# Tanh-GELU feed-forward stage on Trainium2: cube computed on POOL, curve opened on DVE, excess as half less its clip

## The reference, cut to what matters

```
def _qdot(x, w, out_dtype=BF16):
    return jnp.dot(x.astype(E4M3), w.astype(E4M3), preferred_element_type=out_dtype)
ff_gate = _qdot(x, w_gating[0])        # 256 -> 1024
gate_value = jax.nn.gelu(ff_gate)      # tanh form
ff1 = _qdot(x, w_gating[1])            # 256 -> 1024
activations = gate_value * ff1
outputs = _qdot(activations, w_linear) # 1024 -> 256
```

## Time and profile before

| | us |
|---|---|
| median of three runs | 2270.92 |
| lowest and highest | 2260.33, 2270.98 |
| profiled execution | 2276.07 |
| its span | 2274.3 |

### The profile page before, as it was taken

One profiled execution on the slowest core, in us unless ns is written; L12 is line 12 of the kernel. 1 busy time (PEld: TensorE's weight loads), 2 busy tenths in 40 slices (PEclk: granted clock), 3 DMA queues, 4 the chain that ended last, 5 costly groups with the idle time before them and its releaser, 6 DMA issues. The chain is left out here.

```text
span 2274.3 us, 41972 instructions
## 1 busy us (share of the span) xinstructions
PE 1944.8 (86%) x11782; PEld 1303.9 (57%) x11798; DVE 1366.0 (60%) x3452; ACT 1075.4 (47%) x2800; POOL 717.9 (32%) x691
## 2 busy tenths in 40 slices
PE   7999999998998997776899999979856788988665
PEld 4666666665565665544566666635533457777432
DVE  6555665565775354343533344469879547777687
ACT  5544545553333221111344444357778437666576
POOL 3233333230000023343255556523100016666410
PEclk9999999999999888768999999989978889989887
DMA  9960000000000001142477777500010111111100
GB/s 311 288 188 0 0 0 0 0 1 0 0 0 1 1 27 47 44 161 74 117 167 165 168 175 133 124 1 2 1 58 1 62 36 33 29 35 34 31 17 21
DMA packets 145576, 145.10 MB, mean 64 GB/s; under 512 B 49377, under 2 KB 133569, under 8 KB 145345
## 3 DMA queue, kind: packets, MB, share of 16 engines
q1 hardware_dynamic: 122432, 113.81, 17.4%
q0 software_dynamic: 23040, 30.01, 7.7%
HBM read 137.12 MB, written 66.44 MB: 90 GB/s over the span
## 5 line engine op out<-in xcount | busy, mean ns | idle before, releaser
L1684 POOL DMA_INDIRECT expert_sums<-moe_rows_in,moe_to x128 | 198.0, 1547 | 155.7 <-DMA expert_sums<-moe_rows_in,moe_to 100.1
L1757 PE MATMUL moe_gate<-moe_places,moe_xt 128*128 x512 | 176.3, 467 | 2.3 <-issue 1.9
L1947 DVE COPY moe_ht_e<-moe_turned 128x256 f32<-128x256 f32 x128 | 54.4, 425 | 203.2 <-PE moe_turned L1765 192.5
L619 ACT ACTIVATE ga_prob<-ga_score,ga_neg_max 128x128 f32<-128x128 f32 x256 | 99.6, 390 | 145.9 <-DVE ga_neg_max L493 145.9
L3010 POOL TENSOR_TENSOR wa_low<-wa_low,wa_top 128x512 f32<-128x512 f32 x128 | 133.2, 1041 | 97.3 <-DVE wa_top L3214 96.0
L240 POOL TENSOR_TENSOR ga_q_inv<-ga_q_sum,half 128x4 f32<-128x4 f32 x64 | 64.5, 1008 | 304.2 <-DVE ga_q_sum L476 304.2
L2037 POOL TENSOR_TENSOR ln_rstd<-ln_var,half 128x4 f32<-128x4 f32 (+1 forms) x16 | 21.9, 1370 | 367.5 <-DVE ln_var L2033 367.4
L1151 POOL DMA_INDIRECT slot_x<-early x96 | 94.0, 979 | 137.5 <-DVE early L1144 109.5
L3211 DVE SCALAR_TENSOR_TENSOR wa_low<-wa_score,early 128x512 f32<-128x512 f32 x128 | 87.8, 686 | 60.7 <-PE wa_score L3050 58.1
L375 PE MATMUL ga_summed<-ga_wo,ga_out_t 128*128 128x256 f32 x512 | 122.5, 383 | 0.7 <-ACT ga_out_t L627 0.7
L375 PEld LDWEIGHTS ga_summed<-ga_wo,ga_out_t 128*128 128x128 f32 x512 | 98.1, 192 | 40.6 <-issue 29.2
(11 more groups left out here) (480 smaller groups left out, 4967.8 us busy)
## 6 DMA issues: line engine op xcount, KB each, us to landing
moe_places<-in_L_ffn_packed SPq DMA_DIRECT2D x128, 608.0 KB
slot_x<-zeros SPq DMA_DIRECT2D x24, 1076.0 KB, 15.7
moe_rows_in<-slot_x SPq DMA_DIRECT2D x128, 134.5 KB
wa_v<-v_ctx SPq DMA_DIRECT2D x16, 180.0 KB, 3.0
early<-in_L_xattn_Wq SPq DMA_DIRECT2D x5, 512.0 KB, 7.9
x<-in_x SPq DMA_DIRECT2D x4, 512.0 KB, 9.1
ga_wo<-in_L_xattn_Wo SPq DMA_DIRECT2D x1, 2048.0 KB, 14.1
expert_sums<-zeros SPq DMA_DIRECT2D x2, 1024.0 KB, 8.1
```

What stands on the lines that cost most here:

```text
L619: last = act.activation(prob[:, n % 2, part], score[:, n % 2, part], ACT.Exp, bias=neg_max[:, n % 2, h:h + 1], accum_out=total[:, n % 2, h ...
L1684: pool.indirect_dma_start(out=mem.sums[j % SUMS], out_offset=bass.IndirectOffsetOnAxis(ap=to[:, j:j + 1], axis=0), in_=y[:, j, :], in_offs ...
L1757: last = pe.matmul(both[j % 2][:, 0:2 * FE], xt[:, j % 2, c, :], packed[:, place, c * 2 * FE:(c + 1) * 2 * FE].rearrange("p a n -> p (a n) ...
```

## The change

Three edits, all inside `gelu_ffn`, with the same values computed:

1. The cube is no longer made on DVE but on POOL, by sixteen `tensor_tensor` instructions queued ahead of `norm_next.root`. Each waits for `square` of its step, for `part` of two steps before (which reads the buffer that the cube overwrites), and for `gate` of four steps before. DVE's `part` waits for the new semaphore `cubed`, and so does ACT's square of two steps later.
2. `more` is no longer made on ACT but on DVE, by a `tensor_scalar` with two operations, right before `gate`. ACT's tanh now waits for the `more` of two steps before.
3. The excess is now half less its clip: `within` = min(max(half, -120), 120) in one `tensor_scalar` with two operations, and `over` = half - within as a `tensor_tensor`.

```diff
-        curve = signal("curve", 4)
+        curve, cubed = signal("curve", 3), signal("cubed")
...
             @block.gpsimd
             def _(pool):
+                def cubes(n):
+                    pool.wait_ge(squared.sem, squared.at(n))
+                    if n >= 2:
+                        pool.wait_ge(curve.sem, curve.at(n - 2))
+                    if n >= DEEP:
+                        pool.wait_ge(made.sem, made.at(n - DEEP))
+                    pool.tensor_tensor(cube[:, n % 2, :, :], square[:, n % 2, :, :], g[:, n % DEEP, :, :], ALU.mult).then_inc(cubed.sem, 1)
+
+                for n in range(N):
+                    cubes(n)
                 norm_next.root(pool, 0, 0, B - GROUP)
...
                     if n >= 2:
-                        act.wait_ge(curve.sem, curve.at(n - 2))
+                        act.wait_ge(cubed.sem, cubed.at(n - 2))
                     act.wait_ge(g_moved.sem, g_moved.at(n))
                     act.activation(square[:, n % 2, :, :], g[:, n % DEEP, :, :], ACT.Square).then_inc(squared.sem, 1)
...
                 def bend(n):
-                    act.wait_ge(curve.sem, curve.at(n, 3))
+                    act.wait_ge(curve.sem, curve.at(n, 2))
+                    if n >= 2:
+                        act.wait_ge(opened.sem, opened.at(n - 2))
                     act.activation(tanh[:, n % 2, :, :], root[:, n % 2, :, :], ACT.Tanh).then_inc(tanhed.sem, 1)
-                    act.wait_ge(tanhed.sem, tanhed.at(n))
-                    if n >= 2:
-                        act.wait_ge(made.sem, made.at(n - 2))
-                    act.activation(more[:, n % 2, :, :], tanh[:, n % 2, :, :], ACT.Copy, scale=0.5, bias=0.5).then_inc(opened.sem, 1)
...
-                    dve.wait_ge(squared.sem, squared.at(n))
-                    dve.tensor_tensor(of(cube), of(square), here, ALU.mult).then_inc(curve.sem, 1)
+                    dve.wait_ge(cubed.sem, cubed.at(n))
+                    dve.tensor_scalar(of(part), of(cube), CUBE, None, ALU.mult).then_inc(curve.sem, 1)
                     dve.wait_ge(curve.sem, curve.at(n))
-                    dve.tensor_scalar(of(part), of(cube), CUBE, None, ALU.mult).then_inc(curve.sem, 1)
-                    dve.wait_ge(curve.sem, curve.at(n, 1))
...
+                    dve.wait_ge(tanhed.sem, tanhed.at(n))
+                    dve.tensor_scalar(of(more), of(tanh), 0.5, 0.5, ALU.mult, ALU.add).then_inc(opened.sem, 1)
                     dve.wait_ge(opened.sem, opened.at(n))
                     dve.tensor_tensor(of(gate), of(more), g[:, n % DEEP, :, :], ALU.mult).then_inc(made.sem, 1)
...
                     dve.wait_ge(halved.sem, halved.at(n))
-                    dve.tensor_scalar(under[:, n % 2, :, :], half[:, n % 2, :, :], -E4M3_TOP / 2, None, ALU.min).then_inc(excess.sem, 1)
+                    dve.tensor_scalar(within[:, n % 2, :, :], half[:, n % 2, :, :], -E4M3_TOP / 2, E4M3_TOP / 2, ALU.max, ALU.min).then_inc(excess.sem, 1)
...
-                    dve.scalar_tensor_tensor(over[:, q % 2, u * UC:(u + 1) * UC, :], half[:, n % 2, :, :], E4M3_TOP / 2, under[:, n % 2, :, :],
-                                             ALU.max, ALU.add).then_inc(excess.sem, 1)
+                    dve.tensor_tensor(over[:, q % 2, u * UC:(u + 1) * UC, :], half[:, n % 2, :, :], within[:, n % 2, :, :],
+                                      ALU.subtract).then_inc(excess.sem, 1)
```

More of the change, by code:

```diff
@@ L2529, in gelu_ffn @@
         g = beyond.shaped([P, DEEP, UC, GT], BF16)
-        square, cube, part, inner, root, tanh, more, gate, lin, prod, under = (
-            sb(x, [P, 2, UC, GT]) for x in ("square", "cube", "part", "inner", "root", "tanh", "more", "gate", "lin", "prod", "under"))
+        square, cube, part, inner, root, tanh, more, gate, lin, prod, within = (
+            sb(x, [P, 2, UC, GT]) for x in ("square", "cube", "part", "inner", "root", "tanh", "more", "gate", "lin", "prod", "within"))
         half = sb("half", [P, 2, UC, GT], FP8)
@@ L2688, in bend @@
                         dve.wait_ge(tanhed.sem, tanhed.at(n - 2))
-                    dve.wait_ge(curve.sem, curve.at(n, 2))
+                    dve.wait_ge(curve.sem, curve.at(n, 1))
                     dve.tensor_scalar(of(root), of(inner), ROOT, None, ALU.mult).then_inc(curve.sem, 1)
```

## The result

The changed kernel takes 2295.78 us (median of six runs, 2290.20 to 2302.54), the kernel before 2263.87 us beside it (six runs, 2258.92 to 2270.98; three of these are the runs of the first table). The ratio is 1.0133, with a 95% interval of 1.0108 to 1.0159: slower by 30 us of 2264, between 24 and 36. The forecast was +24.8 us and 2296 us. The profiled execution of the changed kernel took 2302.54 us, 26.5 more than that of before.

A forecast was written before the change was run, and what follows sets the result against it. DVE's queue was taken to pace the stage's 16 steps, with ACT 0.3 us behind. 16 x (1.81 - 0.26) = +24.8 us on the 2270.9 us median gave 2295.7, stated as 2296 us, range 2270 to 2312.

The forecast's parts named there:

- (a): DVE's step in `gelu_ffn`: the cube leaves DVE, which gains its slot of 0.72 us a step.
- (b): DVE before `gate`: `more` enters as a bf16 tensor_scalar, DVE loses 0.46 us a step; its wait on tanh costs nothing.
- (c): ACT loses `more`, 1057 ns a step; worth nothing by itself, leaving ACT at about 4.9 us a step.
- (d): Excess on DVE: `within` taken at 685 ns, `over` at 1225, a gain of nothing; the other end would give 8.6 us.
- (e): POOL takes the cube: 2.08 us for 1024 bf16 elements, twice the price of the 512-element f32 row.
- rival 2: POOL's bf16 cube is cheap, 1.04 us, so +8 us, 2279 us in all; chance 0.10.
- (f): POOL's cube and DVE's instructions take turns at SBUF; each cube costs DVE 1.81 us, making the step 7.79 us.
- The handovers: Between POOL and DVE taking turns: give back 0.27 us for each POOL instruction, subtracted from the cube's 2.08.
- Rival 1: bf16 on POOL and DVE do not exclude each other; -4.2 us, 2267, or 2258 with a fast subtraction; chance 0.12.
- Rival 3: POOL runs only when DVE has stopped at `cubed`, nothing overlapped; +31 us, 2302, or 2315 at the dearest cube; chance 0.13.
- (g): What could be late next: POOL's input and ACT's waits met in time, TensorE at 7.2 us a step behind DVE, tail unchanged.

The follow-up runs named there:

- cube_4: Changed kernel with POOL's product cut to 4 of the 1024 elements of each partition, all waits kept; stage 123.32 us, ratio 0.9974 to the kernel before.
- more_only: Kernel before with `more` alone moved from ACT to DVE, POOL idle; stage 131.96 us, ratio 1.0020 (0.9996 to 1.0044).
- cube_only: Kernel before with the cube alone moved to POOL, `more` left on ACT and the excess as it was; stage 146.78 us, ratio 1.0080.
- spare_multiply: Kernel before plus one POOL bf16 multiply of 128x1024 a step that nobody waits for; stage 153.80 us, ratio 1.0110.
- the last two: Kernel before with a sigmoid for root, tanh and `more`, ratio 0.9965; kernel before with scales in square and tanh and `more` on DVE, ratio 0.9960.

## Why the prediction was right

**(a), (b), DVE's own step.** Forecast 5.98 us without POOL; `cube_4` has steps of 5.96 to 5.99, and `more_only` shows the slot of `more` by itself, 6.70 - 6.24 = 0.46. Shown. The wait on tanh cost 1.4 us once, near the end, in place of `gate`'s 1.6.

**(c) ACT's relief is worth nothing by itself.** Shown by `more_only`: ACT loses 1.06 us a step and the stage grows. Together with the cube on POOL it does help: in `cube_only`, where ACT keeps `more`, DVE waits 10.7 us for cubes and for `more`, in the changed kernel 7.4 (6.0 for the first cube and 1.4 for tanh). Of ACT's idle time the forecast was too low. I gave it up to some 2.5 us a step; it has (149.85 - 85.11) / 16 = 4.0, of which the kernel before had 1.7.

**(d) The excess.** `over` 1225 at least, `within` 685 in the median: no gain, as taken. The argument from the pace of fp8 sources gave the right price; what else could set it was not tried, and the third edit had no run of its own.

**(e) POOL's price.** 2.08 taken, 2.12 measured alone. The elements decide and not the bytes, so rival 2 (1.04) is out, and so is 2.91. The estimate of 2.25 from the Trainium skill, GPSIMD Engine Reference, section 3.1, was 0.13 too high for this form.

**(f) Taking turns.** 1.81 us for each cube taken; measured at the instructions hit, it is 1.72 (`root` above) to 1.80 (2226 - 427), and up to 1.92 for `within` and for `finish`'s additions, 1.80 in the mean. The handovers gave back 0.32 where 0.27 was taken, and the cube was 0.04 dearer: two small errors that cancel. The plain steps are 7.70 and 7.78 against 7.79. Rival 1 (no exclusion) is out by `spare_multiply`. Rival 3 (POOL gets in only when DVE stands) is out by the timeline: POOL comes in behind the DVE instruction that is running, and only the first cube is waited for, 6.0 us in place of 3.8. That the loss is the exclusion and not the detour through POOL is shown by `spare_multiply` and `cube_4` together.

**(g) What is late next.** Nothing that reached DVE: `part` waited for POOL once in the stage. ACT ran ahead as argued; it stood for TensorE's `lins` for 27.6 us, but that did not delay DVE. "The tail after the last `over` is as before" was wrong by 1.5 us: DVE waits 2.0 us before the last additions to x, for 3.5 before. What they wait for is the last 16 `downs` matmuls and ACT's copy of them. The same 16 matmuls ran at the lower clock level before and at the higher one after (first line before, second after, columns of the earlier trace rows); what raised the clock in time is not shown.

```profile
1786.02:1789.48 3.46, 3.46 (x16) 2.16 (x16) 0.55 (x5) 0.00 (x0) 2.27 (x1) 0.53 0.00 0
```

```profile
1805.49:1807.39 1.90, 1.90 (x16) 1.46 (x16) 0.54 (x5) 0.00 (x0) 1.21 (x1) 1.00 0.00 0
```

**The sum.** +24.8 forecast for the stage, +23.05 measured. The price of the cubes came out as forecast: 27.1 us on DVE's instructions and 2.2 of longer waiting for the first cube, 29.3 for the forecast's 16 x 1.81 = 29.0. Behind `finish` two cubes fall into one step (12.4 us) and none into the next (5.95), which changes no sum. DVE's own work is 4.2 less, as forecast. Of what is missing, the tail of (g) is 1.5 us.

**The whole time.** By ratio the loss is 30 us (24 to 36), which holds both 24.8 (only just) and the 26.5 of the profiled pair. Outside the stage the two profiles differ by -5.1 us in front of it and +8.6 behind it, where no line was changed; the kernels of the experiments, unchanged there as well, scatter, but for the last two, from 1654 to 1667 us in front and from 476 to 489 behind. I assign that no cause. In `cube_only` and `spare_multiply` the ratio gives less than the stage does (18 and 25 us for 20 and 27). That the median came within 1 us of the 2296 is luck: the base I added to, 2270.9, fell by 7.0 to 2263.9 with three more runs, and the difference of the medians, 31.9, is 7.1 above the forecast.

## What to carry to other kernels

Before giving POOL an elementwise instruction, look at what DVE runs at that moment, not at whether POOL is idle. If POOL's instruction reads SBUF, DVE is the bound and DVE's instructions have two SBUF inputs or run from SBUF to SBUF with a constant, POOL's time comes back almost whole as DVE time (here 1.7 to 1.9 of 2.1 us, to save 0.72). An instruction whose shortest and median durations are normal and whose longest is up by the length of another engine's is the sign, and a spare instruction that nobody waits for tells it from a wait. Where two engines pace a stage within 5% of each other, folding scales into an activation that runs anyway was worth more here than moving work between them; it costs a rounding each time, which has to be allowed.

## What the runs showed of the hardware beyond that

- A POOL multiply costs 1.88 ns an element in bf16, with 1152 ns for 512 elements against 1041 for 512 f32 elements in the earlier trace rows.
- A POOL memset of 2048 bf16 elements (1804 ns) left every DVE tensor_tensor alone and held up the constant-operand instructions that it met, up to 1.99 us in all for a `root` of 0.43.
- POOL's tiny product of 4 elements takes 198 ns alone, but a median of 388 beside DVE. That the rest is waiting for its turn is the reading that fits the other runs; it was not tried by itself.
- DVE's bn_stats ran beside a POOL multiply with neither delayed (`spare_multiply`, 1738.51), once.
